# Second attention in two sides of four query blocks, with maxima three slots back; first attention's row sums rounded and inverted in two halves

## What is computed

```python
# 1. causal attention in bf16: 16 heads of 16; scores/sqrt(16), softmax, values
coef = where(causal, einsum("bhqd,bhkd->bhqk", q, k) / scale, -inf)
att  = einsum("bhqk,bhkd->bhqd", softmax(coef), v);  out = att @ W_out + b_out
# 2. mixture of 16 experts (top 4 of a router), SiLU-gated, f32
# 3. causal "forgetting" attention in f32: 32 heads of 8
f = log_sigmoid(x @ Wf.T + bf);  c = cumsum(f, axis=1)
scores = einsum("bihd,bjhd->bhij", q, k) / sqrt(8) + c[i] - c[j]
p = softmax(where(causal, scores, -inf));  o = (p @ v) @ Wo.T
# 4. gated MLP with int8 weights (1024 wide)
```

## Time and profile before

| | us |
|---|---|
| median of 3 runs (lowest, highest) | 2035.05 (2033.52, 2035.66) |
| profiled execution, its own time | 2035.23 |
| its span in the trace | 2033.3 |
| first attention, about | 58 to 465 |
| qkv1, about | 1142 to 1224 |
| second attention, about | 1224 to 1791 |

### The profile page before, as it was taken

How to read it: one execution, slowest core, us unless ns; L and a number is a source line. 1 busy time by engine, 2 the same in 40 slices (tenths; PEclk the granted TensorE clock), 3 DMA queues, 4 the chain that set the end, 5 groups by cost and what they waited for, 6 DMA issues and landing times. The chain is left out here.

```text
span 2033.3 us, 33699 instructions
## 1 busy us (share of the span) xinstructions
PE 1577.5 (78%) x9152; PEld 840.1 (41%) x9152; DVE 1320.4 (65%) x4019; ACT 934.8 (46%) x2016; POOL 211.2 (10%) x185
## 2 busy tenths in 40 slices
PE   3555555632199999999999466999999999973995
PEld 1121222211167777777776242333333333331564
DVE  4788888856445555555556496877788878635543
ACT  3888888950011111111111342777777777723212
POOL 0000000000111211111120200111111111101000
PEclk9555555555599999999999686999999999976998
DMA  2255565551100000000000031111111111020001
GB/s 83 51 105 101 101 103 104 107 101 23 29 22 14 27 14 27 14 24 16 16 16 1 17 118 52 32 33 33 34 35 33 35 34 36 16 58 19 1 1 42
DMA packets 197985, 87.81 MB, mean 43 GB/s; under 512 B 166288, under 2 KB 182672, under 8 KB 197840
## 3 DMA queue, kind: packets, MB, share of 16 engines
q1 hardware_dynamic: 196624, 84.30, 18.2%
q10 hardware_dynamic: 1216, 2.03, 0.4%
HBM read 35.29 MB, written 13.24 MB: 24 GB/s over the span
## 5 line engine op out<-in xcount | busy, mean ns | idle before, releaser
L833 DVE CUSTOM_DVE_ANT_0 a_unread<-a_row,all_mask 128x512 bf16<-128x512 f32 (+3 forms) x768 | 392.8, 555 | 106.7 <-PE a_row L678 97.2
L785 ACT ACTIVATE a_probs<-a_st 128x512 f32<-128x512 f32 (+3 forms) x768 | 329.3, 495 | 181.1 <-PE a_st L702 135.2
L1222 PE MATMUL moe_gu<-all_xT_bf,moe_parts 128*112 128x512 bf16 x1536 | 344.9, 382 | 17.8 <-POOL moe_parts L1047 17.8
L1259 ACT ACTIVATE moe_th<-moe_gu 112x512 f32<-112x512 f32 x128 | 76.4, 597 | 489.1 <-PE moe_gu L1222 489.1
L678 PE MATMUL a_row<-l_k,a_q 128*128 128x512 bf16 (+3 forms) x768 | 249.0, 341 | 43.3 <-DMA a_q<-in_q_tail 29.2
L1222 PEld LDWEIGHTS moe_gu<-all_xT_bf,moe_parts 128*112 128x112 bf16 x1536 | 201.1, 131 | 147.3 <-POOL moe_parts L1047 17.9
L699 PE MATMUL a_st<-a_q,l_k 128*128 128x512 bf16 (+3 forms) x768 | 250.7, 333 | 12.3 <-ACT a_probs L785 10.8
L1275 DVE SCALAR_TENSOR_TENSOR moe_tmp<-moe_th,moe_gu 112x512 f32<-112x512 f32 x128 | 88.1, 688 | 255.1 <-ACT moe_th L1259 244.0
L1236 PE MATMUL moe_dn<-moe_wd,moe_actT 112*128 112x256 f32 x1024 | 231.4, 379 | 0.0
L1236 PEld LDWEIGHTS moe_dn<-moe_wd,moe_actT 112*128 112x128 f32 x1024 | 194.7, 190 | 30.2
L544 DVE CUSTOM_DVE_ANT_0 a_rows<-a_sc,all_mask 128x128 bf16<-128x128 f32 (+7 forms) x256 | 192.5, 752 | 14.3 <-PE a_sc L467 13.8
(11 more groups left out here) (202 smaller groups left out, 1684.3 us busy)
## 6 DMA issues: line engine op xcount, KB each, us to landing
a_turned_sb<-a_rows SPq DMA_TRANSPOSE x256, 2.6
moe_raw<-in_gate SPq DMA_DIRECT2D x16, 224.0 KB, 3.0
moe_raw<-in_up SPq DMA_DIRECT2D x16, 224.0 KB, 3.3
moe_wd<-in_down SPq DMA_DIRECT2D x16, 224.0 KB, 2.6
a_q<-q_rows SPq DMA_DIRECT2D x96, 32.0 KB, 2.0
q_rows<-qkv_parts SPq DMA_DIRECT2D x4, 768.0 KB, 3.5
k_rows<-qkv_parts SPq DMA_DIRECT2D x4, 768.0 KB, 3.5
l_k<-k_rows SPq DMA_DIRECT2D x64, 48.0 KB
```

Of the source, the lines that this page charges most:

```text
L785: nc.scalar.activation(probs[:, n % PR, 0:w], st[:, n % AHEAD, 0:w], ACT.Exp).then_inc(exp_done, 1)
L833: nc.vector.tensor_tensor_reduce(out=unread[:, i % SLOTS, 0:w], in0=row[:, i % SLOTS, 0:w], in1=mask[:, at:at + w], scale=1.0, scalar=-3e3 ...
L1222: last = nc.tensor.matmul(gu[0:IC, n % 2, i, :], parts[:, j, k // KC, i, k % KC, ch * IC:(ch + 1) * IC], xT[:, k % KC, g * 512:(g + 1) * 512],
```

## The change

**First attention.** The sums are rounded and inverted in two halves: items 0 to 7 at e = 0, items 8 to 15 at e = 6, and `scale` begins at e = 0 instead of 1.

**Second attention.** The query blocks stand in the order ORDER = (1, 2, 5, 6 | 7, 4, 3, 0), two sides of 512 columns, in q, in the scores, in `o` and in the stored output. For kb < 4 one exponential covers both sides of one head (up to 1024 columns); for kb >= 4 one covers both heads of the span of columns that the key block needs. So a unit has 12 exponentials instead of 24; score tiles are two of 1024 columns. `late` and L702 are gone: 28 of the 64 rows of a head's tile, free before, or filled with zeros, now hold steps ("stairs") that put the large negative value on most of the square right of the diagonal, and POOL zeroes what is left after the exponential, by one `affine_select` of 128x2x128 for each kb (8 a unit), for which PE's values wait (`masked`). The values go by kb, in 8 groups, into 32 rows for each (h, side): nothing is added later, and one copy of 128x512 (`copy_out`, L779) and one store of 64 KB replace four copies, POOL's addition and two stores. The row tiles are a free-running ring in which the turned maxima take whatever slot comes (`row_entries`), each entry waiting only for the entry three back. Chunks that don't touch the diagonal (8 of 24) use a plain `tensor_reduce` without the mask. The loop is gone: all 32 units are written out. A unit's q and k come in 4 DMAs of 64 partitions.

**qkv1.** q and k are stored as 8 planes in DRAM in the form that is loaded (6 repeated or plain part planes, two planes of constant tails, some of it c): twice the part data, in three stores a tile. q is made in pieces of 256 or 128 columns because of ORDER. `project_rows` reads and writes in the new order.

```diff
-            def total_rounded(u):
-                dve.wait_ge(summed, NI * (u + 1))
-                nc.vector.tensor_copy(totb[:, u % 2], total[:, u % 2]).then_inc(inv_ready, 1)
+            def total_rounded(u, first, end):
+                dve.wait_ge(summed, NI * u + end)
+                nc.vector.tensor_copy(totb[:, u % 2, first:end], total[:, u % 2, first:end]).then_inc(inv_ready, 1)
...
-                    if e == 1:
-                        total_rounded(u)
-                    if e >= 2:
+                    if e == 0:
+                        total_rounded(u, 0, NI // 2)
+                    if e == NI // 2 - 2:
+                        total_rounded(u, NI // 2, NI)
+                    if e:
                         scale(n)
...
+VALUES = {1: (0,), 3: (1,), 5: (2,), 7: (3,), 9: (4, 5), 11: (6, 7)}
+LATER = ((12, 13), (14, 15), (16, 17), (18, 19), (20, 21), (22, 23),
+         (0, 1), (2,), (TURN, 3), (4, 5, 6), (7, 8, 9), (10, 11))
...
+            for u in range(units):
+                for k in range(NGR):
+                    to_u, to_g = (u, k + 2) if k + 2 < NGR else (u + 1, k + 2 - NGR)
+                    if to_u < units:
+                        scores(to_u, to_g, 0)
+                    for m, what in enumerate(LATER[k]):
+                        to = u + 1 if what == TURN or what >= NC // 2 else u + 2
+                        if to < units:
+                            entry(to, what)
+                        if m == 0 and to_u < units:
+                            scores(to_u, to_g, 1)
+                    for kb in VALUES.get(k, ()):
+                        values(u, kb)
...
+            def causal(u, kb):
+                n = NGR * u + group_of(kb, 1)
+                pool.wait_ge(exp_done, n + 1)
...
+                nc.gpsimd.affine_select(tiles, tiles, [[0, 2], [1, P]], ALU.is_ge, 0.0, base=0,
+                                        channel_multiplier=-1).then_inc(masked, 1)
...
+                if n >= SLOTS:
+                    dve.wait_ge(row_free, n - SLOTS + 1)
+                if lo + w == (qb + 1) * P:
...
+                else:
+                    nc.vector.tensor_reduce(top, tile[:, 0:w], mybir.AxisListType.X, ALU.max).then_inc(row_free, 1)
...
+                if i:
+                    return [(0, 512, tg * 512)]
+                blocks = ORDER[tg % 2 * 4:tg % 2 * 4 + 4]
+                if tg % 2 == 0:
+                    return [(0, 2 * P, tg // 2 * S + blocks[0] * P), (2 * P, 2 * P, tg // 2 * S + blocks[2] * P)]
+                return [(m * P, P, tg // 2 * S + blk * P) for m, blk in enumerate(blocks)]
```

More of the change, by code:

```diff
@@ new lines, in _ @@
+            for u in range(RING):
+                load(sp, u, q_sb[:, u], k_sb[:, u], qk_loaded[u])
+            for u in range(units):
+                if u and u + 3 < units:
+                    sp.wait_ge(st_ready, NGR * u)
+                    load(sp, u + 3, q_sb[:, (u + 3) % RING], k_sb[:, (u + 3) % RING], qk_loaded[(u + 3) % RING])
+                sp.wait_ge(o_copied, u + 1)
+                sp.dma_start(o_rows[u * 4 * HW:(u + 1) * 4 * HW, :], oT[:, u % 2]).then_inc(stored[u % 2], 16)
@@ new lines, in entry, with scores @@
+            def entry(u, what):
+                if what == TURN:
+                    turn_max(u)
+                else:
+                    row_chunk(u, what)
+            def scores(u, g, part):
+                kb, heads = GROUPS[g]
+                n = NGR * u + g
+                if part == 0:
+                    if g == 0:
+                        pe.wait_ge(row_free, entry_of[u, TURN] + 1)
+                    if n >= 2:
+                        pe.wait_ge(exp_done, n - 1)
+                lo, hi = columns_of(kb)
+                if len(heads) == 1:
+                    h, first, end, to = heads[0], max(lo, SIDE * part), min(hi, SIDE * (part + 1)), 0
+                else:
+                    h, first, end, to = part, lo, hi, part * SIDE - lo
+                last = nc.tensor.matmul(st[:, n % 2, to + first:to + end], k_sb[:, u % RING, h, kb * P:(kb + 1) * P],
+                                        q_sb[:, u % RING, first:end], start=True, stop=True)
+                if part == 1:
+                    last.then_inc(st_ready, 1)
@@ new lines, in values @@
+            def values(u, kb):
+                if kb == 0:
+                    pe.wait_ge(v_ready, u + 1)
+                    if u:
+                        pe.wait_ge(o_copied, u)
+                pe.wait_ge(masked, TB * u + kb + 1)
+                for side in range(2):
+                    for h in range(2):
+                        lo, hi, to = columns(kb, h)
+                        first, end = max(lo, SIDE * side), min(hi, SIDE * (side + 1))
+                        if first >= end:
+                            continue
+                        at = HW * (2 * h + side)
+                        last = nc.tensor.matmul(o[at:at + HW, first - SIDE * side:end - SIDE * side],
+                                                v_sb[:, u % RING, kb, h, :],
+                                                probs[:, (NGR * u + group_of(kb, h)) % GR, to + first:to + end],
+                                                start=(kb == 0), stop=(kb >= TB - 2), skip_group_check=True)
+                last.then_inc(pv_done, 1)
@@ L879, in _, with add_max @@
-            rounds(dve, slot)
+            def add_max(u):
+                n = entry_of[u, TURN]
+                dve.wait_ge(row_ready, n + 1)
+                nc.vector.tensor_tensor(out=q_sb[:, u % RING], in0=row[:, n % SLOTS].bitcast(BF16),
+                                        in1=q_sb[:, u % RING], op=ALU.add).then_inc(row_free, 1)
+            for u, what in entries:
+                if what == TURN:
+                    add_max(u)
+                else:
+                    max_of(u, what)
+                    if what == NC - 1:
+                        parts_of_max(u)
@@ L1009, in _ @@
                 dve.wait_ge(y_ready, t + 1)
-                norm.count(t, y)
+                norm.count(tile(t), y)
         @block.tensor
@@ L1371, in _ @@
                     pe.wait_ge(qf_ready, n - 1)
-                for k in range(KC):
-                    last = nc.tensor.matmul(acc[:, n % 2, :], w_sb[:, i, k, ch * P:(ch + 1) * P],
-                                            xT[:, k, tg * 512:(tg + 1) * 512], start=(k == 0), stop=(k == KC - 1))
+                for to, w, at in pieces(i, tg):
+                    for k in range(KC):
+                        last = nc.tensor.matmul(acc[:, n % 2, to:to + w], w_sb[:, i, k, ch * P:(ch + 1) * P],
+                                                xT[:, k, at:at + w], start=(k == 0), stop=(k == KC - 1))
                 last.then_inc(acc_ready, 1)
@@ L1685, in forget_attention @@
+        attention(nc, "a1", units, hd, data + 3, F32, load, k_steps, k_sb, v_units, o_rows, mask, ident_b)
         project_rows(nc, "o1", o_rows, a["wo"], a["of_head"], y, norm)
```

463 lines of the change are left out of this document (196 added, 267 removed).

## The result

The changed kernel takes 1984.0 us (median of 4 runs, 1983.37 to 1985.96) against 2035.3 beside it: a ratio of 0.9751, 95% interval 0.9734 to 0.9768, faster by 51 us.

A forecast was written before the change was run, and what follows sets the result against it. It took SP's queue as next limit in the first attention and PE as pacing the second. From 2035.2 us, -11.5 (first attention), +6.3 (qkv1), -5 (start), -14 (units) and -4.2 (end) gave 2007, range 1985 to 2031.

The forecast's parts named there:

- First attention: First attention: sums in two halves remove DVE's wait, but SP's queue limits the gain; -11.5 us (-8 to -12.5).
- The loop: Second attention: seven periods at round ends take 19.1 us, the others 16.1; writing the loop out is worth 21 us.
- The waits of a unit: Second attention, one unit: PE's 1.4 us of waits, on maxima and ACT, stay about as they are.
- L702: Second attention: removing the mask matmuls takes 0.9 us a unit off PE's work.
- The copy: Second attention, turn of a unit: the output copy between exponentials 0 and 1 makes PE wait, +1.0 us (0 to 2.1).
- The mask on GpSimd: Second attention: POOL's mask between exponential and values takes 0.5 us each, adding waits of 0.2 us a unit.
- The slower rival: Second attention: masks of 2.08 us make POOL the limit, 2044 us; it decides at about 1.6 us each; chance 0.10.
- qkv1: qkv1 stage: q in pieces costs +4.3 us, the last k store and the c store +2; together +6.3 (+3 to +9).
- Start: Start of the second attention: fewer DMAs issue before unit 0, so PE stands less; -5 us (-3 to -7).
- End: End of the second attention: one copy and one store, -2.8 us, and a shorter last unit, -1.4; together -4.2.
- the whole stall of the first attention: Rival, first attention: SP is not the limit, so -34 us in place of -11.5, 1985 us; chance 0.07.
- the case of a unit under 15.4: Rival, second attention: it loses its stalls, units of 15.0 to 15.4 us, 1966 to 1978 us in all; chance 0.13.

## Why the prediction was wrong

- **First attention, right.** -11.5 forecast, -12.0 in the two traces and -9.4 (6 to 13) alone. That the stall of 44 us would mostly not come back, since SP's transpositions and loads were next, is shown by the run without loads.
- **The loop, right in size, partly by luck.** 21 us forecast, 20 measured in the units. I took seven long periods of 19.1 us, one for each round, and 16.1 for all others. The trace has six, of 18.1 to 19.3 us (18.7 on average), worth 16 us, and the other 4 us stand inside the rounds; the two errors nearly cancel.
- **The waits of a unit, the step that failed.** The mechanism was right, its sum was not. From 14.7 of work and 1.4 of waits I made 13.8 of work and 2.5 of waits: the 1.4 that "stay about as they are", +1.0 for the copy, +0.2 for POOL, -0.1 for DVE. PE's work came as forecast (14.75, then 13.90). The waits measured 1.30 before and 1.93 after: 0.92 for the copy, nothing for POOL, and 1.0 of the 1.4 that were to stay. So the unit missed POOL's 0.2, 0.3 of the standing waits and 0.1 of the copy's, less 0.1 of work: 0.48, and 31 of these are 15 us of the 23 (-14 forecast for the units, -29.0 measured). Why the standing waits fell by 0.3 is open: the plain maxima are ruled out (nothing for them), and the ring's new rule kept them from rising by 0.71, but did not take away a wait of the kernel before.
- **L702.** 0.9 forecast for PE's work, and the work fell by 0.85. Put back alone the matmuls cost 0.53 a unit, since 0.35 of them hides in waits.
- **The copy, near.** 1.0 forecast, 0.89 measured, a wait of 0.92 from start to start.
- **The mask on GpSimd, half right.** 0.5 us forecast, 0.406 measured; the 0.2 us a unit for waits was nothing. The first mask starts at 1242.27 as soon as its exponential is done, and all 256 take 0.406 to 0.416, so nothing extra is on the path. The Trainium skill (GPSIMD Engine Reference, 2.1 Instruction dispatch) gives about 6 us for the first call of a freshly loaded kernel, with no visible instruction; POOL stood idle 25.98 us before the first mask, so this trace can't show whether it was paid there. The slower rival had the wrong price. A slow mask does cost time, and before POOL is full, by the delay of one link: three masks in a row cost 33 us.
- **Maxima, plain form.** 0.1 forecast, 0 measured.
- The unit by my terms was 16.1 - 0.9 - 0.1 + 1.0 + 0.2 = 16.3. Start to start it is 16.05 - 0.85 of work + 0.92 for the copy - 0.3 of the other waits = 15.82, as in the trace.
- **qkv1.** +6.3 forecast, +2.6 in the trace. The pieces cost nothing that the run shows in place of 4.3. Their price came from a row at a mean granted clock of 0.64; scaled to 1.00 the 0.207 is 0.13, and the pieces took 0.11. What is left would be the doubled stores and the c store, whose issue took 2.27 us in place of 0.82; I had taken 2 for them; that is argued, since they were not tried apart.
- **Start.** -5 forecast, -4.8 measured.
- **End.** -4.2 forecast, -7.4 in the trace. The store comes 0.66 us after the last values in place of 3.5 (2.9, where 2.8 was forecast), and the last unit itself is 4.2 shorter instead of 1.4. With no maxima beside it, it is a chain of scores, exponentials and values with a wait at each, and twelve exponentials have fewer of them than 24. That reason is argued from the two traces, not tested by itself.
- **The range** went to 1985 for a case that didn't happen (the whole stall of the first attention), and I left the case of a unit under 15.4 outside with 0.13. The true unit lies between that case and my forecast.

## What to carry over

When a wait is moved in a ring of buffers, first look in the trace of the kernel before whether the limiting engine stood there at all. Putting the old rule back into the new kernel prices the rule in the new order; what it cost in the old order stands only in the old trace, and a sum that comes out right can hide two waits that changed places. Read such waits from start to start, since the view hides the short ones. Before a copy is put between two exponentials, see what it waits for: here one position later was worth 30 us, more than the loop. And a duration may only be carried from one stage to another with the granted clock of both beside it.

## What the runs showed of the hardware

GpSimd's affine select of 128x256 f32 in place takes 0.406 us, 1.59 ns an element with its fixed cost, the first one 0.416. Sixteen f32 matmuls of 128 columns take 1.79 us where four of 512 take 1.72, at the same granted clock of 1.00. A plain reduction of 512 columns in PSUM is no faster than adding a mask, taking the maximum and reading it out: 0.60 us from start to start for both. A DMA of both q and k for a head costs SP 0.52 us, about as much as one of them alone (0.42 to 0.57). In the first attention 16 transpositions on SP's queue take 21.2 to 21.8 us, 1.3 each, and set the pace of the stage.
